# Capacity experts: last products as pairs of 64-row products, gate and up products in two banks

## The chip, the cores and the metric

The kernel runs on one core of a Trainium2 chip. It is a raw program: each engine has its own hand-written instruction order, and waits are explicit semaphores. The metric is the device time of one execution in microseconds (us), lower is better. All data are float32.

## The reference, cut to what matters

The program is four transformer-like layers over 8 sequences of 512 tokens with 128 features. The change touches only the last piece, the expert mixture of layer L3. There are 64 experts with hidden width 64, each takes at most 256 token copies (CAP), and every token goes to its two best experts:

```
buf = zeros(E=64, CAP=256, d=128).at[flat_e, pos].set(x_pairs, mode='drop')
h = silu(einsum('ecd,edh->ech', buf, w1)) * einsum('ecd,edh->ech', buf, w3)      # h = 64
y = einsum('ech,ehd->ecd', h, w2)                                               # contraction over 64
routed = (y[flat_e, pos] * top_scores).sum over the two choices
out = shared + routed
```

## The kernel before

The last layer is the function `capacity_mixture`. It has three stages.

The first routes. For each pair of sequences, the tokens' normalized rows are written to a DRAM array `queues` at expert*256+position by indirect DMAs that GpSimd issues (`scatter`, 64 of them, line 2436). Meanwhile SyncE loads the weights: `w13` (gate and up weights, 4 MB) and `w2_pairs` (4 MB, into `big`, lines 2412 and 2413).

The second is the expert loop. It runs over 32 units u, a unit being two experts (a = 0 and 1) with 256 rows each. Per unit, TensorE does, in this order in iteration u:

- T(u): four transposes of the loaded rows X(u) into bank `XP(u)` (line 2727); ScalarE copies them to `XT` (line 2644).
- G(u-1): gate and up products (line 2736), four matmuls with a 128x64 weight tile and 256 moving columns; expert a writes partitions 64a to 64a+63 of the bank `GU`. ScalarE takes a tanh of the gate half (2650), VectorE multiplies twice (2597 and 2601) and leaves `AA`, whose partitions 0 to 63 are the hidden values of expert 0 and 64 to 127 those of expert 1.
- Y(u-3): the last products (line 2747). Two matmuls, one for each 128 of the 256 slots, each with all 128 partitions of `AA` as the stationary operand and 256 columns of `w2` moving. `w2_pairs` holds the weights padded: the columns of expert 0 are zero in partitions 64 to 127 and those of expert 1 are zero in partitions 0 to 63, so one matmul gives both experts' outputs side by side. VectorE scales by 0.5 out of bank `YP(u)` into `Y(u)` (2593), and GpSimd issues the store to `results` (2452).

`DEEP` = 4 is the number of `GU` banks (2 to 5), `ROOM` = 2 that of the other banks. G(v) waits for AA(v-4), Y(v) for AA(v) and for the scaling of v-2.

The third stage gathers two rows for each token back from `results` (64 indirect DMAs, line 2463), and VectorE adds them with their shares (2561).

In the text an "fp32 matmul" of the program shows in the trace as two MATMUL and two LDWEIGHTS instructions (Y: 2 matmuls, x4 in the rows; G: 4 matmuls, x8); a transpose shows as one.

Of the kernel before, what the change touches and what calls it, by code (L numbers as in the profile page):

```python
# [13 lines left out]
F32 = mybir.dt.float32  # L14
I32 = mybir.dt.int32
U32 = mybir.dt.uint32
ALU = mybir.AluOpType
# [3 lines left out]
P = 128  # L21
B, T, D = 8, 512, 128
NC_ = T // P
NT = B * NC_
# [6 lines left out]
CE, CH, CAP = 64, 64, 256  # L31
# [62 lines left out]
class Memory:  # L94


    def __init__(self, ctx, nc, dram):
        self.ctx, self.nc, self.dram = ctx, nc, dram


        self.h_more = self.sb("h", [P, NT + 2 * NC_, D])
        self.h = self.h_more[:, 0:NT, :]
        self.bank = [ctx.enter_context(nc.psum_tensor(f"bank{n}", [P, T], F32)) for n in range(8)]
        self.w = {}
        self.loaded = {}
        self.load_log = []
# [2229 lines left out]
def capacity_mixture(ctx, nc, m):  # L2336
# [4 lines left out]

    w13 = ctx.sb("w13", [P, CE, 2 * CH])
    w13_in, w2_in = ctx.semaphore("loaded_w13"), ctx.semaphore("loaded_w2")
    w2 = m.big[:, NT * D:NT * D + CE // 2 * 2 * D].rearrange("p (q n) -> p q n", n=2 * D)
    place_of = ctx.sb("place", [P, PAIRS, 4 * NC_])
    share = ctx.sb("share", [P, PAIRS, 4 * NC_])
    idx = ctx.sb("cc_idx", [P, PAIRS, 4 * NC_], I32)
# [33 lines left out]
    sg_ps, su_ps, sg_sb, s1_sb, s2_sb, sy_ps, sh_sb = (sig(n, 2) for n in ("g_ps", "u_ps", "g_sb", "s1_sb", "s2_sb", "y_ps", "h_sb"))  # L2381

    sig = named("ce_")
    UN, SLOTS, DEEP, ROOM = CE // 2, 8, 4, 2
    QC = CAP // P
    X = lambda u: m.KM[0][:, u % SLOTS, :]
    Y = lambda u: m.KM[1][:, u % SLOTS, :]
    XT = lambda u: m.XT[u % 2]
    TH = lambda u: m.t512a[u % 2][:, u // 2 % 2 * CAP:(u // 2 % 2 + 1) * CAP]
    AA = lambda u: m.t512b[u % 2][:, u // 2 % 2 * CAP:(u // 2 % 2 + 1) * CAP]  # L2390
# [2 lines left out]
    x_free, xt_ps, xt_sb, gu_ps, th_sb, a_sb = (sig(n) for n in ("x_free", "xt_ps", "xt_sb", "gu_ps", "th_sb", "a_sb"))  # L2393
    aa_sb, y_ps, y_sb = (sig(n) for n in ("aa_sb", "y_ps", "y_sb"))
    XP = lambda u: m.bank[u % 2]
    GU = lambda u: m.bank[2 + u % DEEP]
    YP = lambda u: m.bank[6 + u % 2]
    acf = lambda v: v.rearrange("p (a c f) -> p a c f", a=2, c=QC)
    rows = lambda t, u: t[u * 2 * CAP:(u + 1) * 2 * CAP, :].rearrange("(a p c) d -> p a (c d)", a=2, c=QC)
    nd = lambda v: v.rearrange("p (a n) -> p a n", a=2)  # L2400

# [5 lines left out]
    with nc.Block() as block:  # L2407
# [60 lines left out]
        def _(dve):  # L2468
# [120 lines left out]
            def last_part(u):  # L2589
                dve.wait_ge(y_ps.sem, u + 1)  # L2590
                if u >= SLOTS:
                    dve.wait_ge(y_out[u % SLOTS].sem, 16 * (u // SLOTS))
                nc.vector.tensor_scalar(acf(Y(u)), YP(u)[:, :].rearrange("p (c a f) -> p a c f", a=2, c=QC), 0.5, None, ALU.mult).then_inc(y_sb.sem, 1)

            for u in range(UN):
                dve.wait_ge(th_sb.sem, u + 1)
# [15 lines left out]
        def _(act):  # L2612
# [26 lines left out]
            for u in range(UN + 1):  # L2639
# [5 lines left out]
                if u >= 1:  # L2645
                    v = u - 1
                    act.wait_ge(gu_ps.sem, v + 1)
                    if v >= DEEP:
                        act.wait_ge(aa_sb.sem, v - DEEP + 1)
                    nc.scalar.activation(TH(v), GU(v)[:, 0:CAP], ACT.Tanh, scale=0.5).then_inc(th_sb.sem, 1)  # L2650

        @block.tensor
        def _(pe):
            def gate(i):
                for s in S if i else ():
                    pe.wait_ge(norms[i % 2].ready.sem, norms[i % 2].ready.at(nth(i), s + 1))
                    if i >= 2:
                        pe.wait_ge(sh_sb.sem, sh_sb.at(i - 2, 2))
                    for c in range(NC_):
                        last = nc.tensor.transpose(TB(i, s)[:, c * P:(c + 1) * P], tiles(i, s)[:, c, :], w["ident"][:, :])  # L2660
                    last.then_inc(gx_ps.sem, 1)
                for s in S:
                    if i:
                        pe.wait_ge(gx_sb.sem, gx_sb.at(i - 1, s + 1))
                    for c in range(NC_):
                        n = s * NC_ + c
                        last = nc.tensor.matmul(LG(i)[:, n * CE:(n + 1) * CE], GX[i % 2][s][:, c * P:(c + 1) * P], w["c_gate"][:, :], start=True, stop=True)
                last.then_inc(lg_ps.sem, 1)

            def count(i):  # L2670
                pe.wait_ge(cu_sb.sem, i + 1)
                if i >= 2:
                    pe.wait_ge(s2_sb.sem, s2_sb.at(i - 2, 2))
                into = ne(COUNT(i)[:, :])
                nc.tensor.matmul(into, w["earlier"][:, :], en(M)[:, :, 1:R9].rearrange("p e n -> p n e"), start=True, stop=False)  # L2675
                nc.tensor.matmul(into, w["ones"][:, 0:P], en(INCL)[:, :, 0:R8].rearrange("p e n -> p n e"), start=False, stop=True).then_inc(pos_ps.sem, 1)  # L2676

            def shared_hidden(i):
                for s in S:
                    if s == 0:  # L2680
                        if i:
                            pe.wait_ge(gx_sb.sem, gx_sb.at(i - 1, 2))
                    else:
                        pe.wait_ge(sc_sb.sem, i + 1)
                    nc.tensor.matmul(SHARED_G(i, s)[:, :], w["sw1"][:, :], GX[i % 2][s][:, :], start=True, stop=True).then_inc(sg_ps.sem, 1)
                for s in S:
                    if s == 1:
                        pe.wait_ge(cst.sem, cst.at(i, 2))
                    nc.tensor.matmul(SHARED_U(i, s)[:, :], w["sw3"][:, :], GX[i % 2][s][:, :], start=True, stop=True).then_inc(su_ps.sem, 1)

            def shared_out(i):
                for s in S:
                    pe.wait_ge(s2_sb.sem, s2_sb.at(i, s + 1))
                    for c in range(NC_):
                        last = nc.tensor.matmul(SHARED_Y(i, s)[:, c * P:(c + 1) * P], SG[s][:, c * P:(c + 1) * P], w["sw2"][:, :], start=True, stop=True)
                    last.then_inc(sy_ps.sem, 1)

            pe.wait_ge(m.loaded["c_gate"], 16)
            gate(0)
            pe.wait_ge(m.loaded["earlier"], 16)  # L2700
            count(0)
            gate(1)
            for name in ("sw1", "sw3", "sw2"):
                pe.wait_ge(m.loaded[name], 16)
            shared_hidden(0)
            shared_out(0)
            gate(2)
            count(1)
            for i in range(1, PAIRS - 1):
                shared_hidden(i)  # L2710
                count(i + 1)
                shared_out(i)
                if i + 2 < PAIRS:
                    gate(i + 2)
            shared_hidden(PAIRS - 1)
            shared_out(PAIRS - 1)
            pe.wait_ge(sh_sb.sem, sh_sb.at(PAIRS - 1, 2))

            pe.wait_ge(w13_in, 16)
            pe.wait_ge(w2_in, 16)  # L2720
            for u in range(UN + 3):
                if u < UN:
                    pe.wait_ge(x_in[u % SLOTS].sem, 16 * (u // SLOTS + 1))
                    if u >= ROOM:
                        pe.wait_ge(xt_sb.sem, u - ROOM + 1)
                    for n in range(2 * QC):
                        last = nc.tensor.transpose(XP(u)[:, n * P:(n + 1) * P], X(u)[:, n * P:(n + 1) * P], w["ident"][:, :])  # L2727
                    last.then_inc(xt_ps.sem, 1)
                if 1 <= u <= UN:
                    v = u - 1  # L2730
                    pe.wait_ge(xt_sb.sem, v + 1)
                    if v >= DEEP:
                        pe.wait_ge(aa_sb.sem, v - DEEP + 1)
                    for k in range(2):
                        for a in range(2):
                            last = nc.tensor.matmul(GU(v)[a * CH:(a + 1) * CH, k * CAP:(k + 1) * CAP], w13[:, 2 * v + a, k * CH:(k + 1) * CH],  # L2736
                                                    XT(v)[:, a * CAP:(a + 1) * CAP], start=True, stop=True)
                            if k == a == 0:
                                last.then_inc(x_free.sem, 1)
                    last.then_inc(gu_ps.sem, 1)  # L2740
                if u >= 3:
                    v = u - 3
                    pe.wait_ge(aa_sb.sem, v + 1)
                    if v >= ROOM:
                        pe.wait_ge(y_sb.sem, v - ROOM + 1)
                    for c in range(QC):
                        last = nc.tensor.matmul(YP(v)[:, c * 2 * D:(c + 1) * 2 * D], AA(v)[:, c * P:(c + 1) * P], w2[:, v, :], start=True, stop=True)  # L2747
                    last.then_inc(y_ps.sem, 1)


# [59 lines left out]
def laid_out(inputs):  # L2810

    a = {k: np.asarray(v) for k, v in inputs.items()}
    row = lambda x: np.ascontiguousarray(x)
    out = dict(shape_constants())
# [25 lines left out]
    p = np.arange(P)  # L2840
# [13 lines left out]
    q = np.arange(B * 8)  # L2854
# [24 lines left out]
        out[n] = row(a["L3_ffn_" + n])  # L2879
    out["w13"] = row(np.concatenate([a["L3_ffn_w1"], a["L3_ffn_w3"]], axis=2).transpose(1, 0, 2).reshape(P, -1))  # L2880
    w2 = a["L3_ffn_w2"].reshape(CE // 2, 2, CH, D)
    pairs = np.zeros((2, CH, CE // 2, 2, D), w2.dtype)
    for e in range(2):
        pairs[e, :, :, e] = w2[:, e].transpose(1, 0, 2)
    out["w2_pairs"] = pairs.reshape(P, -1)
    return out


# [13 lines left out]
```

## Time and profile before

| what | value |
|---|---|
| time, median of 3 runs | 2267.86 us (2266.97 to 2274.65) |
| span of the profiled execution | 2301.6 us |
| mean granted TensorE clock over the span | 0.898 |
| expert loop, first transpose to last scaling | 2125.45 to 2208.96 us |
| instructions of PE, PEld, DVE, ACT, POOL | 11676, 11676, 4911, 1459, 392 |

The profile gives no other time of its own execution than its span, which is 33.7 us above the median of the runs. PE is TensorE's matmuls, PEld its weight loads, DVE VectorE, ACT ScalarE, POOL GpSimd, SP SyncE. A duration of a matmul row is its own latency, neighbours overlap, so groups are timed here from the start of one group to the start of the next. PEclk is the granted clock of TensorE: 1.00 is 2.4 GHz and 0.50 is 1.2 GHz. "128*64 128x256" is a weight tile of 128 rows and 64 columns with 256 moving columns on 128 rows.

### The profile page before, as it was taken

Reading aid. Unit: us, or ns where it says so; the run is one execution under the profiler, and the core shown is the slowest. Engines: PE = TensorE matmul, PEld = TensorE weight load, DVE = VectorE, ACT = ScalarE, POOL = GpSimd, SP = SyncE. Lnnn points to the kernel's source line nnn. Section 1 sums busy time; section 2 is a strip of 40 time slices with the busy share of each in tenths; the row PEclk is TensorE's granted clock in tenths of the full one; section 3 lists DMA queues with packets and bytes.
Section 4 is the critical chain, followed back from the end, with each engine's and each line's share of the span. In section 5 each row is a group of like instructions: output and inputs, shape, how many; then the busy total and the mean of one; then the engine's idle time right before and its main releaser. Section 6 shows DMA issues by size and latency. Waiting matters only on the chain. (4 is left out here: it accounts for less than half of the span.)

```text
span 2301.6 us, 31594 instructions
## 1 busy us (share of the span) xinstructions
PE 1858.3 (81%) x11676; PEld 957.7 (42%) x11676; DVE 1747.6 (76%) x4911; ACT 1317.0 (57%) x1459; POOL 327.8 (14%) x392
## 2 busy tenths in 40 slices
PE   5998998988766688999999999889999888652930
PEld 2565755766421123344433334433344553231620
DVE  3667557667777789999999999999999789763532
ACT  0223122231237999999999999999999612100310
POOL 6000022010343000000000000000000000173256
PEclk9879999787777999999999999999999999776975
DMA  5501000000001100000000000000000000221632
GB/s 163 180 1 38 16 2 14 1 1 1 1 0 35 65 1 1 1 1 1 1 1 1 1 1 1 1 1 1 1 1 1 1 1 0 106 92 53 208 96 73
DMA packets 39658, 67.08 MB, mean 29 GB/s; under 512 B 7744, under 2 KB 27728, under 8 KB 38736
## 3 DMA queue, kind: packets, MB, share of 16 engines
q1 hardware_dynamic: 30768, 41.96, 5.4%
q0 software_dynamic: 8736, 23.10, 3.2%
q8 instruction: 93, 1.52, 0.3%
q14 instruction: 61, 0.50, 0.1%
HBM read 39.87 MB, written 23.07 MB: 27 GB/s over the span
## 5 line engine op out<-in xcount | busy, mean ns | idle before, releaser
L1942 ACT ACTIVATE KM<-KM 128x2048 f32<-128x2048 f32 x290 | 538.9, 1909 | 8.0 <-DVE KM L1765 8.0
L1765 DVE TENSOR_SCALAR KM<-big 128x512 f32<-128x512 f32 x1160 | 480.8, 484 | 38.7 <-PE bank L2080 32.9
L2080 PE MATMUL bank<-KM,w_a_wa 128*32 128x512 f32 x2736 | 379.6, 629 | 91.1 <-ACT KM L1942 69.7
L189 POOL TENSOR_TENSOR nrstd<-nrstd,minus_half 128x4 f32<-128x4 f32 (+1 forms) x80 | 82.4, 1050 | 1745.9 <-DVE nrstd L166 1745.5
L1942 ACT ACTIVATE aa_args<-aa_args 128x2048 f32<-128x2048 f32 x142 | 266.1, 1909 | 1.5 <-DVE aa_args L1765 1.5
L1765 DVE TENSOR_SCALAR aa_args<-big 128x512 f32<-128x512 f32 x568 | 236.3, 484 | 13.8 <-PE bank L2080 13.2
L2080 PE MATMUL bank<-aa_args,w_a_wa 128*32 128x512 f32 x1360 | 188.2, 627 | 42.2 <-ACT aa_args L1942 28.5
L2080 PEld LDWEIGHTS bank<-KM,w_a_wa 128*32 128x32 f32 x2736 | 54.8, 109 | 243.0 <-ACT KM L1942 140.6
L2052 PE MATMUL bank<-XT,rf_wgu 128*128 128x256 f32 x512 | 143.9, 404 | 0.0
L2046 PE MATMUL bank<-XT,rf_wgu 128*128 128x256 f32 x512 | 142.2, 400 | 0.8 <-DVE ST L1837 0.8
L1939 ACT ACTIVATE KM<-big 128x512 f32<-128x512 f32 x208 | 132.8, 717 | 0.0
L2052 PEld LDWEIGHTS bank<-XT,rf_wgu 128*128 128x128 f32 x512 | 88.0, 191 | 96.8 <-issue 77.3
L2046 PEld LDWEIGHTS bank<-XT,rf_wgu 128*128 128x128 f32 x512 | 87.5, 189 | 93.4 <-issue 84.7
L1837 DVE SCALAR_TENSOR_TENSOR ST<-ST,bank 128x512 f32<-128x512 f32 x128 | 87.8, 686 | 43.0 <-ACT ST L1932 42.7
L1932 ACT ACTIVATE ST<-bank 128x512 f32<-128x512 f32 x128 | 75.9, 593 | 46.3 <-PE bank L2052 46.3
L2040 PEld LDWEIGHTS bank<-rf_wd,ST 128*128 128x128 f32 x512 | 62.1, 191 | 51.3 <-issue 48.3
L2040 PEld LDWEIGHTS bank<-rf_wd,t512b 128*128 128x128 f32 x512 | 62.3, 191 | 37.8 <-issue 36.9
L1850 DVE SCALAR_TENSOR_TENSOR h<-bank,rf_w,h 128x128 f32<-128x128 f32 x256 | 77.7, 348 | 0.0
L594 ACT COPY KM<-bank 128x512 f32<-128x512 f32 x32 | 17.2, 593 | 104.5 <-PE bank L754 104.5
L2080 PEld LDWEIGHTS bank<-aa_args,w_a_wa 128*32 128x32 f32 x1360 | 27.2, 109 | 119.3 <-ACT aa_args L1942 69.1
L2040 PE MATMUL bank<-rf_wd,ST 128*128 128x128 f32 x512 | 73.8, 287 | 1.8 <-DVE ST L1843 1.7
L2326 PE MATMUL bank<-big,w_ident 128*128 128x512 f32 x128 | 58.8, 619 | 18.9 <-DVE big L2221 18.9
(405 smaller groups left out, 3120.6 us busy)
## 6 DMA issues: line engine op xcount, KB each, us to landing
queues<-zeros SPq DMA_DIRECT2D x1, 8192.0 KB, 24.1
KM<-queues SPq DMA_DIRECT2D x32, 256.0 KB, 3.0
results<-KM POOLq DMA_DIRECT2D x32, 256.0 KB, 3.4
w<-in_w SPq DMA_DIRECT2D x1, 4096.0 KB
big<-in_w_pairs SPq DMA_DIRECT2D x1, 4096.0 KB
mf_tv<-in_task_W SPq DMA_DIRECT2D x1, 2048.0 KB, 10.4
la_v<-in_task_W SPq DMA_DIRECT2D x1, 2048.0 KB, 8.6
big<-XN SPq DMA_DIRECT2D x8, 256.0 KB, 2.7
```

What stands on the lines that cost most here:

```text
L189: self.nc.gpsimd.tensor_tensor(self.m.nrstd[s][:, 0:self.tiles], self.m.nrstd[s][:, 0:self.tiles], self.m.minus_half[:, 0:self.tiles], ALU ...
L1765: last = nc.vector.tensor_scalar(ARG(n, step)[:, cc, :], KU[:, i * T:(i + 1) * T], q, None, ALU.add)
L1837: nc.vector.scalar_tensor_tensor(TH(e), TH(e), 1.0, GATE(e)[:, :], ALU.add, ALU.mult).then_inc(a1_sb.sem, 1)
L1850: last = nc.vector.scalar_tensor_tensor(h, OUT(e)[:, s * D:(s + 1) * D], WT[:, s, e:e + 1], h, ALU.mult, ALU.add)
L1932: nc.scalar.activation(TH(e), GATE(e)[:, :], ACT.Tanh, scale=0.5).then_inc(th_sb.sem, 1)
L1939: last = nc.scalar.activation(ARG(n, step)[:, cc, :], KU[:, i * T:(i + 1) * T], ACT.Tanh, bias=query(n, step, cc))
L1942: last = nc.scalar.activation(ARG(n, step), ARG(n, step), ACT.Tanh)
L2040: last = nc.tensor.matmul(OUT(e)[:, s * D:(s + 1) * D], AC(e)[:, o:o + P], wd[:, e, a, :], start=a == 0, stop=a == HB - 1)
L2046: last = nc.tensor.matmul(LIFT(e)[:, a * TOK:(a + 1) * TOK], wgu[:, e, 1, a, :], XMT[parity][:, 0:TOK], start=True, stop=True)
L2052: last = nc.tensor.matmul(GATE(e)[:, a * TOK:(a + 1) * TOK], wgu[:, e, 0, a, :], XMT[parity][:, 0:TOK], start=True, stop=True)
L2080: last = nc.tensor.matmul(m.bank[g][32 * cc:32 * cc + 32, :], w["a_wa"][:, 30 - 2 * k:62 - 2 * k], ARG(n, step)[:, cc, :], start=k == 0, s ...
L2326: last = nc.tensor.matmul(OUT[half][:, :].rearrange("p (l d) -> p l d", d=D), w["ident"][:, :], every[:, :, k, :], start=k == 0, stop=k == ...
```

## The change

The four `GU` banks become two (banks 2 and 3), and banks 4 to 7 become two pairs of neighbouring banks for the outputs. Y(v) is now four matmuls instead of two: for each 128 slots, expert 0 uses array rows 0 to 63 (its half of `AA` and its own `w2`), writing the first bank of the pair, and expert 1 uses rows 64 to 127, writing the second bank. The moving operand has 128 columns instead of 256, and the weights are stored without the zeros, 2 MB instead of 4 MB. VectorE reads one pair of banks in one instruction. G(v) waits for AA(v-2) instead of AA(v-4).

```diff
-        self.bank = [ctx.enter_context(nc.psum_tensor(f"bank{n}", [P, T], F32)) for n in range(8)]
+        self.bank = [ctx.enter_context(nc.psum_tensor(f"bank{n}", [P, T], F32)) for n in range(4)]
+        self.bank_pair = [ctx.enter_context(nc.psum_tensor(f"bank_pair{n}", [P, 2, T], F32)) for n in range(2)]
+        self.bank += [pair[:, n, :] for pair in self.bank_pair for n in range(2)]
...
-    w2 = m.big[:, NT * D:NT * D + CE // 2 * 2 * D].rearrange("p (q n) -> p q n", n=2 * D)
+    w2 = m.big[:, NT * D:NT * D + CE // 2 * D].rearrange("p (q n) -> p q n", n=D)
...
-    UN, SLOTS, DEEP, ROOM = CE // 2, 8, 4, 2
+    UN, SLOTS, DEEP, GATED, ROOM = CE // 2, 8, 4, 2, 2
...
-    GU = lambda u: m.bank[2 + u % DEEP]
-    YP = lambda u: m.bank[6 + u % 2]
+    GU = lambda u: m.bank[2 + u % GATED]
+    YP = lambda u: m.bank_pair[u % 2][:, :, 0:QC * D]
...
-                nc.vector.tensor_scalar(acf(Y(u)), YP(u)[:, :].rearrange("p (c a f) -> p a c f", a=2, c=QC), 0.5, None, ALU.mult).then_inc(y_sb.sem, 1)
+                nc.vector.tensor_scalar(nd(Y(u)), YP(u), 0.5, None, ALU.mult).then_inc(y_sb.sem, 1)
...
-                    if v >= DEEP:
-                        pe.wait_ge(aa_sb.sem, v - DEEP + 1)
+                    if v >= GATED:
+                        pe.wait_ge(aa_sb.sem, v - GATED + 1)
...
                     for c in range(QC):
-                        last = nc.tensor.matmul(YP(v)[:, c * 2 * D:(c + 1) * 2 * D], AA(v)[:, c * P:(c + 1) * P], w2[:, v, :], start=True, stop=True)
+                        for a in range(2):
+                            last = nc.tensor.matmul(YP(v)[:, a, c * D:(c + 1) * D], AA(v)[a * CH:(a + 1) * CH, c * P:(c + 1) * P],
+                                                    w2[a * CH:(a + 1) * CH, v, :], start=True, stop=True)
...
-    pairs = np.zeros((2, CH, CE // 2, 2, D), w2.dtype)
-    for e in range(2):
-        pairs[e, :, :, e] = w2[:, e].transpose(1, 0, 2)
-    out["w2_pairs"] = pairs.reshape(P, -1)
+    out["w2_pairs"] = row(w2.transpose(1, 2, 0, 3).reshape(P, -1))
```

TensorE's order in the middle of the expert loop before (KM0 holds X, t512b is `AA`, the last number is how many matmuls):

```order
L2747 MATMUL bank6<-big,t512b0 128x256 x2
L2727 MATMUL bank0<-w_ident_1,KM0 128x128 x4
L2736 MATMUL bank5<-XT1,w13 64x256 x4
L2747 MATMUL bank7<-big,t512b1 128x256 x2
L2727 MATMUL bank1<-w_ident_1,KM0 128x128 x4
L2736 MATMUL bank2<-XT0,w13 64x256 x4
```

The same place in the changed kernel:

```order
L2749 MATMUL bank_pair0<-big,t512b0 128x128 x4
L2728 MATMUL bank0<-w_ident_1,KM0 128x128 x4
L2737 MATMUL bank3<-XT1,w13 64x256 x4
L2749 MATMUL bank_pair1<-big,t512b1 128x128 x4
L2728 MATMUL bank1<-w_ident_1,KM0 128x128 x4
L2737 MATMUL bank2<-XT0,w13 64x256 x4
```

The order of the groups is the same; the last products are four instead of two, with half the columns, and the gate and up products alternate between banks 2 and 3.

TensorE's last rows of the program before:

```order
L2747 MATMUL bank6<-big,t512b0 128x256 x2
L2736 MATMUL bank5<-XT1,w13 64x256 x4
L2747 MATMUL bank7<-big,t512b1 128x256 x2
L2747 MATMUL bank6<-big,t512b0 128x256 x2
L2747 MATMUL bank7<-big,t512b1 128x256 x2
```

and in the changed kernel:

```order
L2749 MATMUL bank_pair0<-big,t512b0 128x128 x4
L2737 MATMUL bank3<-XT1,w13 64x256 x4
L2749 MATMUL bank_pair1<-big,t512b1 128x128 x4
L2749 MATMUL bank_pair0<-big,t512b0 128x128 x4
L2749 MATMUL bank_pair1<-big,t512b1 128x128 x4
```

Here too only the size and number of the last products differ: Y(28) stands in front of G(31), and Y(29), Y(30) and Y(31) follow it.

## Rows read from the trace of the kernel before

**Rows 1.** Chain that ended last, 1985 to 2151: start us, us, what.
```profile
2063.02 21.74 another core or an unknown queue
...
2122.67 2.65 DMA KM<-queues
2125.32 0.14 issue
2125.45 1.94 PE bank L2727 x8
2127.39 1.91 PE bank L2736 x8
```
**Rows 2.** The same chain, 2203 to 2215.
```profile
2203.91 1.04 PE bank L2736 x8
...
2206.28 0.70 DVE KM L2593
2206.98 0.14 issue
2207.12 1.12 PE bank L2747 x4
2208.23 0.02 issue
2208.26 0.70 DVE KM L2593
```
**Rows 3.** Timeline of PE, 2129 to 2134: start us, us, engine, what.
```profile
2130.85 0.66 PE L2727 MATMUL bank<-w_ident,KM 128*128 128x128 f32 x4
2131.44 1.08 PE L2736 MATMUL bank<-XT,w 128*64 128x256 f32 x8
2132.45 1.13 PE L2747 MATMUL bank<-big,t512b 128*128 128x256 f32 x4
2133.42 0.60 PE L2727 MATMUL bank<-w_ident,KM 128*128 128x128 f32 x4
2133.95 0.44 PE L2736 MATMUL bank<-XT,w 128*64 128x256 f32 x2
```
**Rows 4.** Timeline of all engines, 2160.5 to 2166.5.
```profile
2162.59 1.13 PE L2747 MATMUL bank<-big,t512b 128*128 128x256 f32 x4
2162.71 0.38 ACT L2650 ACTIVATE t512a<-bank 128x256 f32<-128x256 f32 x1 [0.44 <-PE bank L2736]
2163.13 0.42 DVE L2597 SCALAR_TENSOR_TENSOR t512a<-t512a,bank 128x256 f32<-128x256 f32 x1 [1.03 <-ACT t512a L2650]
2163.58 0.42 DVE L2601 TENSOR_TENSOR t512b<-t512a,bank 128x256 f32<-128x256 f32 x1
2163.92 0.68 DVE L2593 TENSOR_SCALAR KM<-bank 128x512 f32<-128x512 f32 x1
```
**Rows 5.** Tile bank, 2132 to 2204: durations ns min/median/max, first and last start.
```profile
L2727 PE MATMUL bank<-w_ident,KM x112: 272/273/273, 2133.4 to 2201.6; 128*128 128x128 f32 x112
```
**Rows 6.** Timeline of PE, 88.9 to 91.1 (layer L0).
```profile
89.11 0.94 PE L754 MATMUL bank<-t512a,ST 32*128 32x128 f32 x12
89.97 1.09 PE L671 MATMUL bank<-w_ident,XN 128*128 128x128 f32 x8
```
**Rows 7.** Timeline of PEld, 88.9 to 90.2, and line 754's weight loads (min/median/max ns).
```profile
89.11 0.75 PEld L754 LDWEIGHTS bank<-t512a,ST 32*128 32x128 f32 x12 [0.17 <-issue]
...
L754 PEld LDWEIGHTS bank<-t512a,ST x96: 181/187/267, 84.5 to 218.4; 32*128 32x128 f32 x96
```
**Rows 8.** Timeline of PE, 440 to 470 (layer L1).
```profile
444.73 9.64 PE L1401 MATMUL bank<-KM,t512b 32*128 32x256 f32 x48 [1.69 <-DVE big L1077]
```
**Rows 9.** Windows: length, busy us (instructions) of PE, PEclk, DMA share, GB/s.
```profile
85.00:95.00 10.00, 10.00 (x101) 1.00 0.15 51
...
446.50:456.80 10.30, 10.30 (x86) 0.50 0.01 2
```
**Rows 10.** Timeline of PE, 105 to 166 (layer L0).
```profile
137.74 1.65 PE L754 MATMUL bank<-ST 32*128 32x128 f32 x12
139.32 1.97 PE L775 MATMUL bank<-w_ident,mf_x 128*128 128x128 f32 x8
```
**Rows 11.** Windows: length, busy us of PE, PEld, DVE, ACT, POOL, PEclk, DMA share, GB/s.
```profile
2010.00:2020.00 10.00, 8.48 (x49) 5.79 (x47) 9.59 (x39) 2.87 (x5) 5.93 (x6) 1.00 0.98 418
2020.00:2030.00 10.00, 5.44 (x24) 5.06 (x24) 9.79 (x53) 1.77 (x3) 8.25 (x8) 0.68 0.18 64
...
2170.00:2180.00 10.00, 10.00 (x66) 6.65 (x64) 5.78 (x12) 3.88 (x8) 2.81 (x5) 1.00 0.66 211
```

More of the change, by code:

```diff
@@ L2395, in capacity_mixture @@
     XP = lambda u: m.bank[u % 2]
-    GU = lambda u: m.bank[2 + u % DEEP]
-    YP = lambda u: m.bank[6 + u % 2]
-    acf = lambda v: v.rearrange("p (a c f) -> p a c f", a=2, c=QC)
+    GU = lambda u: m.bank[2 + u % GATED]
+    YP = lambda u: m.bank_pair[u % 2][:, :, 0:QC * D]
     rows = lambda t, u: t[u * 2 * CAP:(u + 1) * 2 * CAP, :].rearrange("(a p c) d -> p a (c d)", a=2, c=QC)
```

## The prediction

> **What bounds the kernel now.** I read the chain that ended last first, because it says which engine's time is the program's. From 2125.45 on it goes through TensorE alone [rows 1], unit after unit, up to G(31); then it passes ScalarE and VectorE once, Y(31), a scaling and a store, and the gathers start [rows 2]. So the expert loop is TensorE's, and what a unit takes there counts once for each unit. The timeline of PE gives the parts, from group start to group start [rows 3]: Y to T is 2133.42 - 2132.45 = 0.97 us, T behind Y is 0.53, G is 2132.45 - 2131.44 = 1.01. That makes 2.51 us a unit, and TensorE never idles. The windows agree: 10.00 of 10.00 us busy, at clock 1.00, VectorE 5.78 and ScalarE 3.88 [rows 11]. The 112 transposes behind a Y are 28 groups, in 68.2 us, that is 27 periods and a bit: 2.51 again [rows 5].
>
> **The change, part by part.**
>
> *Y itself.* The full-array Y takes 0.97 us. No 64-row tile stands in the trace. The nearest is line 754: six matmuls (x12) with 32-row tiles, 128 weight columns and 128 moving columns, that alternate between two row groups and two banks, as the new Y does with 64 rows. Its group takes 89.97 - 89.11 = 0.86 us, entered from a group of 64-column tiles and left into full-array transposes [rows 6], the same two neighbours that Y has. Its twelve weight loads begin within 0.75 - 0.19 = 0.56 us [rows 7]; one load lasts 0.19. If the loads go one by one, eleven steps give 0.05 us each; in pairs, five steps of 0.11. Either way two instructions cost 0.11 us or less, so the new Y, eight instructions, is 0.86 - 2 x 0.11 = 0.64 us: 0.33 less than now.
>
> *What follows Y.* Before, T followed Y in the same 128*128 shape and took 0.53 us. Now it follows another shape. T behind G, which also changes shape, takes 2131.44 - 2130.85 = 0.59 [rows 3]. So T costs 0.06 more. The drain in front of T is already in the 0.64, since rows 6 are measured up to the next group's start.
>
> On the change of shape, the rows show that 0.06 and whatever stands in the 0.86. The Trainium skill, "TensorEngine Tiling (Array Packing)", section Key Properties, says that changing the tiling mode drains the engine, which speaks against this change: it makes three changes a unit out of two. By this trace the whole price is inside the numbers above.
>
> *Sum of a unit.* 0.64 + 0.59 + 1.01 = 2.24 us against 2.51, 0.27 less. 28 units have a Y and a T behind it: 28 x 0.27 = 7.6 us. Y(28) is followed by G(31), which changes shape anyway: 0.33. Y(29) and Y(30) lie beside the ScalarE and VectorE work behind G(31), and cost nothing on the path; cover gone, they would cost 0.64 each, but the scaling that Y(31) waits for comes after the last multiplication in any case [rows 2]. Y(31) is on the path, 0.33 less. The total is 8.2 us less.
>
> *Two GU banks instead of four.* G(v+2) now waits for AA(v). Counting from a Y start that follows G(v), AA is there at 2163.58 + 0.42 - 2162.59 = 1.41 us [rows 4]. G(v+2) begins two periods less one G later, 2 x 2.24 - 1.01 = 3.47 us. The wait has 2.06 us of room and costs nothing. Behind the waiting G would stand Y, then T and so ScalarE's copy; they get no later. If the room were gone, each late 0.1 us of AA would cost 3.0 us over 30 units.
>
> *VectorE.* The scaling reads 512 values from PSUM now from two banks instead of one; I take its 0.68 us. VectorE does 0.42 + 0.42 + 0.68 = 1.52 us a unit, which the 1.03 us of idle time in front of it [rows 4] shrinks to 0.76 at 2.24. Not a bound; for that the scaling would have to take twice as long.
>
> *Transfers.* A unit loads and stores 0.52 MB; at 2.24 us that is 236 GB/s against 211 now at a DMA share of 0.66 [rows 11]: some 0.74, and eight X buffers lie ahead. Hidden. The weight load is 2 MB shorter, some 5 us at 418 GB/s, but the load is over in the window before 2030 anyway [rows 11] and TensorE needs it at 2125: nothing.
>
> Bounds of the unknown, the row-tiled Y. Below: four pair steps of 0.11 = 0.45 and T at its old 0.53, so 1.99 a unit, 0.52 less, 15.6 us in all. Above: the tiles do not overlap, next rival. I take 0.64, since rows 6 are the same shape but for the rows used.
>
> **The rivals.**
>
> *The halves do not run together (slightly slower).* Line 754's group needs 0.86 - 0.56 = 0.30 us beside its steps [rows 6, 7]; eight instructions one after the other are seven steps of 0.11 more, 1.07 us, 0.10 above the old Y, and T is still 0.06 more: +0.16 a unit, +4.5 over 28 and 0.2 for Y(28) and Y(31), about 2273. For it: no 64-row tile is in the trace. Against it: rows 6 and 7. It decides from a Y group of 0.91 us on, where the gain is gone. The weight loads are the likeliest cause: their number doubles. The Trainium skill, "TensorE: Matmul & The Clock Gate", section LDWEIGHTS, says that a load costs by its columns, not its rows, about 107 ns for 128, so that eight one by one would be 0.85 us (an estimate from that page) and would leave no gain; by rows 7 loads of two row groups overlap, and four pairs are the count.
>
> *The clock falls (clearly slower).* In layer L1, 48 instructions of 32-row tiles in a row took 9.64 us [rows 8] with TensorE busy all the time, at clock 0.50 [rows 9]. So a busy TensorE that uses part of its rows can have the low clock, 1.2 GHz. At 0.50 G is 1.91 us, T 0.97 (1.94 for two) [rows 1], and the new Y, from 139.32 - 137.74 = 1.58 for twelve [rows 10] less two steps at twice 0.11, is 1.14: 4.02 a unit, +1.51 over 28, some 2310. It decides from 15% of the units on. Against it: the stretch 85 to 95 in layer L0, with line 754 and others of that shape between full ones, held 1.00 [rows 9], and here the two halves together use all rows and Y is only 0.64 of 2.24.
>
> *The unnamed wait before the loop changes.* For 21.7 us from 2063 the chain waits for something it cannot name [rows 1], while GpSimd scatters. If the shorter weight load took that away, the time would be some 20 us less, about 2240 with the loop's gain. Against it: the load was over before 2030, more than 30 us earlier [rows 11].
>
> *The full gain.* If changing shape costs nothing, 15.6 us less, 2252.
>
> **How the numbers follow.** The profile's span should go from 2301.6 to 2293.4, and the runs, which lie 33.7 us below the profile, from 2267.9 to 2259.7, 0.36% less. Chances: forecast 0.74 (its own range 2255 to 2264), halves not together 0.09 (2273), clock 0.06 (2310), unnamed wait 0.06 (2240), full gain 0.05 (2252). The range 2252 to 2273 leaves out the clock and the unnamed wait, 0.12. What a measurement of this kernel can tell from no change is about 0.5%, 11.3 us; the forecast lies inside it. Faster by more: unnamed wait 0.06, full gain 0.05, and 0.07 of the forecast's edge: 0.18. Slower by more: the clock, 0.06. The rest, 0.76, is within.
>
> **What would show it.** Line 2749 groups begin 0.64 us before the T behind them, in pairs of close starts; T behind Y 0.59; period 2.24; clock 1.00 from 2130 to the end of the loop; TensorE still busy 10.00 of 10.00 with no wait for `AA`; VectorE's scaling 0.68 us; first gather some 8 us earlier, behind a loop that begins at the same time. Wrong would be: a Y of 0.9 or more, a second level of the clock in the loop, or another start of the loop.

## The result, and the profile after

The changed kernel takes 2264.38 us (median of 20 runs) against 2271.05 for the kernel before: ratio 0.9975, 95% interval 0.9966 to 0.9984, so 3.6 to 7.7 us faster. The quotient of the two medians is 0.9971, inside that interval. Forecast were 8.2 us less, 0.9964 and a time of 2259.7 us. Two repeats gave 0.9971 (0.9959 to 0.9983) and 0.9967 (0.9947 to 0.9988).

The timeline of PE of the changed kernel, from its first transpose on, answers to [rows 1] and [rows 3]:

```profile
2095.42 1.94 PE L2728 MATMUL bank<-w_ident,KM 128*128 128x128 f32 x8 [19.61 <-DMA KM<-queues]
2097.29 1.98 PE L2737 MATMUL bank<-XT,w 128*64 128x256 f32 x8
...
2102.43 0.71 PE L2749 MATMUL bank_pair<-big,t512b 64*128 64x128 f32 x8
2103.07 0.66 PE L2728 MATMUL bank<-w_ident,KM 128*128 128x128 f32 x4
2103.66 1.08 PE L2737 MATMUL bank<-XT,w 128*64 128x256 f32 x8
2104.68 0.71 PE L2749 MATMUL bank_pair<-big,t512b 64*128 64x128 f32 x8
2105.32 0.66 PE L2728 MATMUL bank<-w_ident,KM 128*128 128x128 f32 x4
```

Read from start to start: Y 2103.07 - 2102.43 = 0.64 us (0.97 before), T 0.59 (0.53), G 1.02 (1.01). The period is 2104.68 - 2102.43 = 2.25 us against 2.51. The lines of the other engines in one unit, to be held against [rows 4]:

```profile
2113.66 0.72 PE L2749 MATMUL bank_pair<-big,t512b 64*128 64x128 f32 x8
2113.72 0.71 POOL L2453 DMA_DIRECT2D results<-KM  x1 [1.54 <-DVE KM L2594]
2113.78 0.38 ACT L2651 ACTIVATE t512a<-bank 128x256 f32<-128x256 f32 x1 [0.44 <-PE bank L2737]
2114.20 0.42 DVE L2598 SCALAR_TENSOR_TENSOR t512a<-t512a,bank 128x256 f32<-128x256 f32 x1 [0.77 <-ACT t512a L2651]
...
2114.65 0.42 DVE L2602 TENSOR_TENSOR t512b<-t512a,bank 128x256 f32<-128x256 f32 x1
...
2114.99 0.68 DVE L2594 TENSOR_SCALAR KM<-bank_pair 128x512 f32<-128x512 f32 x1
```

VectorE's idle time in front of its first product has shrunk from 1.03 to 0.77 us, and its instructions last as long as before: the scaling out of two banks takes the same 0.68 us. A window of the loop (columns as in [rows 11]):

```profile
2120.00:2130.00 10.00, 10.00 (x94) 6.25 (x90) 6.01 (x14) 4.35 (x10) 3.42 (x5) 1.00 0.72 235
```

TensorE is still busy all the time, at clock 1.00; the DMA share is 0.72.

**The two spans don't tell the gain.** The profiled spans are 2301.6 us before and 2261.7 after, 39.9 us apart, and most of that has nothing to do with the change. The 64 scatters and the 64 gathers, before and then after (min/median/max ns, first and last start):

```profile
L2436 POOL DMA_INDIRECT queues<-big,cr_sidx x64: 956/962/1366, 2015.1 to 2120.4; - x64
L2463 POOL DMA_INDIRECT KM<-results,cc_idx x64: 943/947/1027, 2212.7 to 2291.7; - x64
```
```profile
L2437 POOL DMA_INDIRECT queues<-big,cr_sidx x64: 954/958/1371, 2005.5 to 2090.3; - x64
L2464 POOL DMA_INDIRECT KM<-results,cc_idx x64: 940/945/1092, 2174.8 to 2253.7; - x64
```

The first scatter already comes 9.6 us sooner, and so does the issue of the weight load (1989.74 against 1999.31), which is the first instruction that differs. A second profile of the changed kernel has its first scatter at 2011.8, so this part varies without any change. The scatters take 105.3 us in one and 84.8 in the other: that is the unnamed wait of [rows 1]. Only what lies between the first transpose and the first gather is the change: 2212.68 - 2125.45 = 87.2 us before, 2174.77 - 2095.42 = 79.35 after, 7.9 us less. In the tables below this stretch is called loop time.

The end of the loop after, from the chain that ended last, answers to [rows 2]:

```profile
2166.05 1.04 PE bank L2737 x8
...
2168.42 0.70 DVE KM L2594
2169.12 0.28 issue
2169.40 1.42 POOL results L2453 x2
2170.82 0.17 issue
2170.99 2.89 DMA results<-KM
```

What follows the scaling of Y(29) at 2168.42 is now GpSimd, which issues the stores of units 29 and 30 one after the other in 1.42 us, and then the last one. The chain passes Y(31) by, but only just: the last scaling starts at 2170.01, 0.98 us before the last store is issued, and in the kernel before it was 0.98 us too (2208.26 to 2209.24). The last scaling and the last store of the changed kernel (timeline), then the last store of the kernel before (chain):

```profile
2170.01 0.69 DVE L2594 TENSOR_SCALAR KM<-bank_pair 128x512 f32<-128x512 f32 x1 [0.30 <-PE bank_pair L2749]
2170.99 0.71 POOL L2453 DMA_DIRECT2D results<-KM  x1 [0.17 <-issue]
```
```profile
2208.96 0.28 issue
2209.24 2.54 DMA results<-KM
```

From issue to landing the last store took 2.54 us and now takes 2.89. So from the last scaling's start to the first gather it was 4.42 us (2208.26 to 2212.68) and is 4.76 (2170.01 to 2174.77).

### The profile page after: what moved, and what is told of

It is laid out like the page before. It is cut to its first block and busy times, and to the rows that moved or that the text cites. A ratio compares the mean times of both kernels' runs of the same rounds, so it can differ in the third digit from the quotient of the medians.

```text
span 2261.7 us, 31852 instructions
## 1 busy us (share of the span) xinstructions
PE 1845.4 (82%) x11804; PEld 950.2 (42%) x11804; DVE 1746.0 (77%) x4911; ACT 1316.9 (58%) x1459; POOL 328.4 (15%) x392
## 5 line engine op out<-in xcount | busy, mean ns | idle before, releaser
L2048 PE MATMUL bank_pair<-XT,rf_wgu 128*128 128x256 f32 x320 | 88.3, 398 | 0.8 <-DVE ST L1839 0.8
L2054 PE MATMUL bank_pair<-XT,rf_wgu 128*128 128x256 f32 x320 | 88.2, 398 | 0.0
L2042 PEld LDWEIGHTS bank_pair<-rf_wd,ST 128*128 128x128 f32 x512 | 62.1, 191 | 51.3 <-issue 48.3
L596 ACT COPY KM<-bank_pair 128x512 f32<-128x512 f32 x32 | 17.2, 593 | 105.1 <-PE bank_pair L756 105.1
L2042 PEld LDWEIGHTS bank_pair<-rf_wd,t512b 128*128 128x128 f32 x512 | 62.3, 191 | 37.8 <-issue 36.9
L2048 PEld LDWEIGHTS bank_pair<-XT,rf_wgu 128*128 128x128 f32 x320 | 54.8, 189 | 54.2 <-issue 48.6
L1852 DVE SCALAR_TENSOR_TENSOR h<-bank_pair,rf_w,h 128x128 f32<-128x128 f32 x256 | 77.0, 341 | 0.0
L2054 PEld LDWEIGHTS bank_pair<-XT,rf_wgu 128*128 128x128 f32 x320 | 54.4, 189 | 52.8 <-issue 36.0
L2042 PE MATMUL bank_pair<-rf_wd,ST 128*128 128x128 f32 x512 | 73.8, 287 | 1.8 <-DVE ST L1845 1.7
L2328 PE MATMUL bank_pair<-big,w_ident 128*128 128x512 f32 x128 | 58.8, 619 | 18.9 <-DVE big L2223 18.9
L2042 PE MATMUL bank_pair<-rf_wd,t512b 128*128 128x128 f32 x512 | 72.3, 284 | 0.0
L1941 ACT ACTIVATE aa_args<-big 128x512 f32<-128x512 f32 x112 | 71.4, 716 | 0.0
```

Of the source, the lines that this page charges most:

```text
L1852: last = nc.vector.scalar_tensor_tensor(h, OUT(e)[:, s * D:(s + 1) * D], WT[:, s, e:e + 1], h, ALU.mult, ALU.add)
L1941: last = nc.scalar.activation(ARG(n, step)[:, cc, :], KU[:, i * T:(i + 1) * T], ACT.Tanh, bias=query(n, step, cc))
L2042: last = nc.tensor.matmul(OUT(e)[:, s * D:(s + 1) * D], AC(e)[:, o:o + P], wd[:, e, a, :], start=a == 0, stop=a == HB - 1)
L2048: last = nc.tensor.matmul(LIFT(e)[:, a * TOK:(a + 1) * TOK], wgu[:, e, 1, a, :], XMT[parity][:, 0:TOK], start=True, stop=True)
L2054: last = nc.tensor.matmul(GATE(e)[:, a * TOK:(a + 1) * TOK], wgu[:, e, 0, a, :], XMT[parity][:, 0:TOK], start=True, stop=True)
L2328: last = nc.tensor.matmul(OUT[half][:, :].rearrange("p (l d) -> p l d", d=D), w["ident"][:, :], every[:, :, k, :], start=k == 0, stop=k == ...
```

## The experiments

Each is compared with the kernel before on the same chip, except one half, which has a single run. After the first result there were three comparisons, each on another chip; the kernel before took 2271, 2292 and 2298 us in them.

| kernel | ratio to before, 95% interval | loop time, us | scatters, us |
|---|---|---|---|
| before, first profile | | 87.2 | 105.3 |
| before again | 1.0009, 0.9984 to 1.0034 | 88.3 | 99.5 |
| before, two gate banks | 1.0004, 0.9991 to 1.0017 | 87.2 | 84.8 |
| before, two by two | 0.9998, 0.9976 to 1.0021 | 85.2 | 101.3 |
| changed | 0.9975, 0.9966 to 0.9984 | 79.4 | 84.8 |
| changed, second time | 0.9971, 0.9959 to 0.9983 | 79.3 | 84.8 |
| changed, third time | 0.9967, 0.9947 to 0.9988 | 80.3 | 99.8 |
| changed, halves in turn | 0.9976, 0.9961 to 0.9990 | 80.5 | 84.8 |
| changed, long load | 0.9947, 0.9925 to 0.9969 | 79.6 | 101.3 |
| changed, long load, second time | 0.9968, 0.9942 to 0.9993 | 79.3 | 105.2 |
| changed, one half (one run) | | 79.7 | 101.0 |
| changed, two by two | 0.9949, 0.9933 to 0.9965 | 73.7 | 84.8 |
| changed, two by two, second time | 0.9947, 0.9922 to 0.9972 | 73.5 | 105.1 |

Two loop times among those near 79.4 stand out. With the halves in turn (80.5) the last store took 3.81 us to land instead of 2.89. In the changed kernel's third profile (80.3) the clock rose later, so that its third and fourth group took 1.04 and 1.53 us instead of 0.61 and 1.02.

**The changed kernel again.** Expected:

> The changed kernel itself, once more. If the gain is the expert loop's alone, the profile again has a period of 2.25 us, a loop that ends 8.2 us sooner after its own start than in the profile of before (2125.45 to 2208.96), and the runs are 7.9 us faster (0.65 us of the loop's and the tail's difference being given back at most). If something outside the loop gives back part of it, the runs stay near 5.7 us. The 20 us wait in the scatters of the first profile: if the shorter weight load removed it, it is absent in this profile as in the first one of the changed kernel; if it comes and goes, it says nothing.

The loop is the same to 0.1 us, and the runs gave 6.6 us less. The scatters' wait is absent again, but see the next one.

**Two gate banks alone.** The edit in the kernel before:

```diff
-    UN, SLOTS, DEEP, ROOM = CE // 2, 8, 4, 2
+    UN, SLOTS, DEEP, GATED, ROOM = CE // 2, 8, 4, 2, 2
...
-    GU = lambda u: m.bank[2 + u % DEEP]
+    GU = lambda u: m.bank[2 + u % GATED]
...
-                    if v >= DEEP:
-                        pe.wait_ge(aa_sb.sem, v - DEEP + 1)
+                    if v >= GATED:
+                        pe.wait_ge(aa_sb.sem, v - GATED + 1)
```

> The kernel before with only one part of the change: gate and up products in two banks, G(v) waits for AA(v-2). My theory: the wait has about 2 us of room, so the loop's period stays 2.51 us and the time is within 2 us of before. Rival: the wait bites, TensorE shows idle time in front of the gate products and the period grows; at 0.1 us a unit that is 3 us.

Loop time 87.2 as before and a ratio of 1.0004: the two banks cost nothing in the loop, and nothing in the time that the interval (2 us less to 4 us more) can show. The timeline of PE of this kernel:

```profile
2105.95 1.13 PE L2747 MATMUL bank<-big,t512b 128*128 128x256 f32 x4
2106.91 0.60 PE L2727 MATMUL bank<-w_ident,KM 128*128 128x128 f32 x4
2107.44 1.08 PE L2736 MATMUL bank<-XT,w 128*64 128x256 f32 x8
2108.46 1.13 PE L2747 MATMUL bank<-big,t512b 128*128 128x256 f32 x4
```

2.51 us from Y to Y, no idle time. It also has the padded 4 MB load, and its scatters took 84.8 us: so the unnamed wait does not belong to that load.

**The halves in turn.** The edit in the changed kernel:

```diff
-                    for c in range(QC):
-                        for a in range(2):
+                    for a in range(2):
+                        for c in range(QC):
```

> The changed kernel with the four last products in another order: both of expert 0 (rows 0 to 63) and then both of expert 1, so that row groups alternate once and not at each matmul. If only neighbours of different row groups overlap, then most of the eight instructions go one after the other: a last-product group of about 1.0 us instead of 0.64, period about 2.6 us, some 10 us slower than the changed kernel, 2 us or more slower than before. If the overlap comes from the smaller tiles whatever their order, the group stays 0.64 and the time is that of the changed kernel.

It is the changed kernel's time: 2163.12 to 2163.77 is 0.65 us for a Y group in its chain, and the ratio is 0.9976. My expectation of 1.0 us fell. The order leaves open whether row groups overlap in any order, or whether a 64-row instruction is simply cheap. The next kernel tells these apart.

**One half alone.** The edit in the changed kernel, which leaves out expert 1's last products and with them half of the routed outputs:

```diff
-                        for a in range(2):
+                        for a in range(1):
                             last = nc.tensor.matmul(YP(v)[:, a, c * D:(c + 1) * D], AA(v)[a * CH:(a + 1) * CH, c * P:(c + 1) * P],
```

> The changed kernel without expert 1's last products: only the two matmuls of rows 0 to 63 are left of each four (half of the routed outputs are left out). It asks how the eight instructions of the last products come to 0.64 us. Theory: two row groups run side by side, each instruction takes 0.11 us in its own. Then four instructions of one group take as long as the eight of two, the group stays about 0.64 us and the period 2.25. Rival, which the unchanged time of the other order allows: a 64-row instruction costs 0.055 us by itself, whatever runs beside it; then the group falls to about 0.42 us and the period to 2.03.

The timeline of PE of this kernel:

```profile
2142.00 0.71 PE L2749 MATMUL bank_pair<-big,t512b 64*128 64x128 f32 x4
2142.64 0.66 PE L2728 MATMUL bank<-w_ident,KM 128*128 128x128 f32 x4
2143.23 1.08 PE L2737 MATMUL bank<-XT,w 128*64 128x256 f32 x8
2144.24 0.71 PE L2749 MATMUL bank_pair<-big,t512b 64*128 64x128 f32 x4
```

Four instructions of one row group take the same 0.64 us as eight of two. An instruction is not cheap by itself; the second half costs nothing because it runs beside the first. Windows of 0.08 and 0.1 us inside one Y group, of line 2749 alone, with the count of instructions under way (in brackets, PE first), bear it out, for one half:

```profile
2142.05:2142.15 0.10, 0.10 (x1) 0.10 (x2) 1.00 0.55 225
```

and for the halves in turn:

```profile
2109.00:2109.10 0.10, 0.10 (x2) 0.10 (x4) 1.00 1.00 410
2109.20:2109.28 0.08, 0.08 (x4) 0.08 (x4) 1.00 0.04 0
```

Right at the start of its group the kernel with the halves in turn has two matmuls under way where one half has one (the changed kernel has two as well). The rows don't say which expert a matmul belongs to. But expert 0's four instructions alone never put a second one under way there, so the second is taken to be expert 1's: it did not wait for the end of expert 0's, although it stands behind all of them in the program.

**The long load.** The edit in the changed kernel:

```diff
-    w2 = m.big[:, NT * D:NT * D + CE // 2 * D].rearrange("p (q n) -> p q n", n=D)
+    w2_more = m.big[:, NT * D:NT * D + CE // 2 * 2 * D]
+    w2 = w2_more[:, 0:CE // 2 * D].rearrange("p (q n) -> p q n", n=D)
...
-            sp.dma_start(w2.rearrange("p q n -> p (q n)"), m.dram["w2_pairs"]).then_inc(w2_in, 16)
+            sp.dma_start(w2_more, m.dram["w2_pairs"]).then_inc(w2_in, 16)
...
-    out["w2_pairs"] = row(w2.transpose(1, 2, 0, 3).reshape(P, -1))
+    out["w2_pairs"] = row(np.concatenate([w2.transpose(1, 2, 0, 3).reshape(P, -1), np.zeros((P, CE // 2 * D), w2.dtype)], axis=1))
```

> The changed kernel with the weight load of the last products padded back to 4 MB by zeros behind the weights, which nothing reads. If the load's size matters to the time, or if it decides the 20 us wait that the first profile of before shows in the scatters, this kernel is slower than the changed one by some us and may show that wait. My theory: the load is over long before it is needed, the time is that of the changed kernel within 2 us, and the wait is absent.

It ran on another chip, where before took 2292.36 us instead of 2271. The ratio of 0.9947 would be 12 us, more than the changed kernel had brought, but its loop time is 79.6 us. So it was put beside the changed kernel in one comparison:

> The changed kernel a third time. From its first transpose to the first gather it took 79.4 us in both profiles, 7.9 us less than the 87.2 of before, yet the runs showed 5.7 and 6.6 us. If the loop's gain is the whole effect, the ratio is near 0.9965 and the three results together cover it. If about 2 us are given back outside the loop, it is near 0.9975 again.

> The changed kernel with the 4 MB load again, now beside the changed kernel in one comparison. On the chip of its first run it was 12 us faster than before, with a wait in the scatters that all four kernels of that call showed. If the load's size does nothing, its ratio equals that of the changed kernel within 0.002. If the shorter load costs something in the stage before the loop, this one is the faster of the two by 2 us or more.

0.9967 and 0.9968. The length of the load does nothing that these intervals, some 5 us to each side, can see; the loop times are 80.3 and 79.3, apart by the clock at the start as said above. And the 0.9947 before was more than the loop can give; it is not explained. The wait in the scatters was there, 99.8 and 105.2 us.

**Before again.** On the chip of the first long load:

> The kernel before itself, as a measure of what no change looks like: a ratio of 1.000 with an interval of about 0.0015 to each side. Its profile shows whether the 21.7 us wait in the scatters belongs to this kernel: if yes, it is there again; if it comes and goes, it is absent and the span is near 2270 us.

The ratio is 1.0009, with an interval of 0.0025 to each side where 0.0015 was expected, and the scatters took 99.5 us. The wait is in all seven profiles of the two slower comparisons and in none of the four of the first, whatever the kernel: it goes with the chip or the time of the run, not with the change.

**Two units at a time.** TensorE's loop of the changed kernel, with the same three steps as functions:

```diff
-            for u in range(UN + 3):
...
+            for j in range(0, UN + 4, 2):
+                for step, lag in ((turn, 0), (gate_up, 2), (down, 4)):
+                    for v in (j - lag, j - lag + 1):
+                        if 0 <= v < UN:
+                            step(v)
```

> The changed kernel with TensorE's loop over two units at a time: T T, G G, Y Y instead of T, G, Y. Tile shapes change three times for two units instead of six. By the rows: T T 0.59 + 4 x 0.109 = 1.03, G G 1.01 + 0.86 = 1.87, Y Y 0.64 + 0.45 = 1.09, together 3.99 us for two units against 4.50, so 0.25 us less a unit, about 8 us less than the changed kernel and 14 to 16 less than before. Rival: the bursts make TensorE wait for AA or XT, since G of the second unit needs VectorE's last product sooner; then idle time shows in front of G and the gain is less than half of that.

> The two-by-two order with 64-row last products again, beside the changed kernel in one comparison. From the first transpose to the first gather its profile showed 73.7 us against 79.4. Theory: 5.7 us faster than the changed kernel, ratio to before near 0.994. Rival: the gain over the changed kernel is chance, then it is within 2 us of it.

2259.63 us and a ratio of 0.9949, and in the second comparison 0.9947. It beats the kernel before. Against the changed kernel beside it the medians are 5.2 us lower (2259.63 and 2264.78) and 7.6 us lower (2281.9 and 2289.46); the intervals of the two kernels overlap, a little in the first comparison and more in the second, so the size of this gain is loose. The loop times are 5.7 and 6.8 us apart. Its timeline of PE, from the start and in the middle of the loop:

```profile
2096.81 1.94 PE L2727 MATMUL bank<-w_ident,KM 128*128 128x128 f32 x8 [19.52 <-DMA KM<-queues]
2099.32 1.78 PE L2727 MATMUL bank<-w_ident,KM 128*128 128x128 f32 x8 [0.57 <-DMA KM<-queues]
2101.03 1.95 PE L2736 MATMUL bank<-XT,w 128*64 128x256 f32 x16
2103.16 0.63 PE L2727 MATMUL bank<-w_ident,KM 128*128 128x128 f32 x4 [0.19 <-ACT XT L2645]
...
2110.45 1.16 PE L2748 MATMUL bank_pair<-big,t512b 64*128 64x128 f32 x16
2111.54 1.09 PE L2727 MATMUL bank<-w_ident,KM 128*128 128x128 f32 x8
2112.57 1.95 PE L2736 MATMUL bank<-XT,w 128*64 128x256 f32 x16
2114.44 1.16 PE L2748 MATMUL bank_pair<-big,t512b 64*128 64x128 f32 x16
```

2114.44 - 2110.45 = 3.99 us for two units, as worked out, and no idle time in the middle. The loop time is 73.7, so 5.7 us less than the changed kernel and not 8. The 8 us counted a saving for every unit, but from the first pair of last products (2106.46) to the last pair that has transposes in front of it (2158.37) there are 13 periods, worth 13 x 0.51 = 6.6 us. At the start TensorE waits 0.57 us for the second pair's transfer and 0.19 and 0.23 us for ScalarE's copies, with only half of the first units' work behind it. At the end it waits 0.20, 0.44 and 0.77 us for VectorE, where the changed kernel waits once, 1.05 us.

The same order in the kernel before:

> The kernel before (full-array last products, padded weights, four gate banks) with the two-by-two order T T, G G, Y Y. By the rows: T T behind Y of the same shape 0.53 + 4 x 0.109 = 0.97, G G 1.87, Y Y 0.97 + 4 x 0.215 = 1.83, together 4.67 us for two units against 5.03, 0.18 us less a unit: about 5.5 us less than before. That is less than the 11.6 us of the same order with row tiles, so the two parts add up. Rival: the order alone is what brought the 11.6 us, then this one gets near it.

Its period is 4.68 us, worked out as 4.67 (from its timeline):

```profile
2136.45 1.99 PE L2746 MATMUL bank<-big,t512b 128*128 128x256 f32 x8
2138.28 1.04 PE L2726 MATMUL bank<-w_ident,KM 128*128 128x128 f32 x8
2139.25 1.95 PE L2735 MATMUL bank<-XT,w 128*64 128x256 f32 x16
2141.13 1.99 PE L2746 MATMUL bank<-big,t512b 128*128 128x256 f32 x8
```

but the loop time is 85.2, only 2.0 to 3.1 us less than before, and the ratio 0.9998 shows no gain; its interval, some 5 us to each side, can't tell 2 us from none. The two-unit start costs most of the rest (the window's columns as in [rows 11]):

```profile
2120.24 1.94 PE L2726 MATMUL bank<-w_ident,KM 128*128 128x128 f32 x8 [18.90 <-DMA KM<-queues]
2122.74 1.97 PE L2726 MATMUL bank<-w_ident,KM 128*128 128x128 f32 x8 [0.55 <-DMA KM<-queues]
2124.64 3.65 PE L2735 MATMUL bank<-XT,w 128*64 128x256 f32 x16
```
```profile
2124.70:2128.20 3.50, 3.50 (x17) 1.66 (x16) 0.84 (x2) 0.86 (x2) 0.00 (x0) 0.51 0.47 149
```

Sixteen gate and up instructions took 3.65 us here at the clock's low level, where in the other kernel they took 1.95. When the clock rises is not the same in every execution (before again has a loop time of 88.3 instead of 87.2 us; its third group, a T, took 1.04 us instead of 0.61), so a part of this is chance. In the profiles at least, the order alone does not bring what it brings together with row tiles: with them each unit has three changes of shape to save on, without them two.

## Why the prediction was right, point by point

The mechanism came out as forecast, term by term. The number did so less well: 2264.38 us lies just outside the forecast's own range (2255 to 2264) and inside the wide one.

- **The new Y, 0.64 us.** Measured 0.64. The 32-row group of layer L0 with the same neighbours [rows 6, 7] carried over to 64 rows to the hundredth. I did not need to know there whether its instructions ran in pairs; one half alone shows that two row groups run side by side, at 0.11 us an instruction in each.
- **T behind another shape, 0.06 more.** Measured 0.59 against 0.53. The third change of shape costs this and the drain inside the 0.64. The two-by-two order, which halves the changes, took 3.99 us for two units instead of 4.50.
- **28 units and two more Ys, 8.2 us.** From the first transpose to the last scaling's start it was 2208.26 - 2125.45 = 82.8 us and is 74.6 (2170.01 - 2095.42): 8.2 us less. This sum was right, with small errors that cancel: up to Y(28) it was 7.4 us (forecast 7.6), for Y(28) 0.4 and from G(31) to the last scaling 0.4 (0.33 each).
- **The tail.** Here the prediction left something out. It credited 0.33 us for Y(31) and carried the store and the first gather over unchanged. But the last store takes 2.89 us to land instead of 2.54, and so 0.34 us are given back; the loop time fell by 7.9 us. This is no chance of one profile: from the last scaling's start to the first gather it is 4.4 us in all four profiles with full-array last products, 4.7 to 4.9 in eight with 64-row ones and 5.7 in the ninth. GpSimd's pause before this store has shrunk from 0.55 to 0.17 us, so the last stores follow each other more closely and may share the queue's time; no run tried that.
- **Two GU banks, VectorE, transfers: nothing.** Right, by the kernel with two gate banks (1.0004), the unchanged 0.68 us of the scaling, and DMA share 0.72 (forecast 0.74) with TensorE busy throughout.
- **The rivals.** The halves do run together, whatever their order. Behind the start of the loop the clock stayed 1.00. The unnamed wait does not depend on the load. Changing shape is not free.
- **A sign of being wrong that came.** "Another start of the loop" was one, and the loop did start 30.0 us sooner (2095.42 against 2125.45). It did not come from the change: 20.5 us of it are the scatters' wait, which is absent from the kernel with two gate banks too and present in later profiles of the changed kernel, and 9.6 us lie before the first scatter.
- **The size.** 7.9 us would be a ratio of 0.9965. The three measurements gave 0.9975, 0.9971 and 0.9967; the second and third intervals hold 0.9965, the first ends just short of it at 0.9966. No stage of the profiles is seen to give back the 1 to 2 us that lie between, but the stage before the first scatter differs by 6.3 us between two profiles of the changed kernel, so the profiles can't rule it out. Whether they are there at all stays open. Of the 4.7 us between the forecast time of 2259.7 and the 2264.38 measured, 3.2 are the kernel before itself: its median was 2267.86 in three runs and 2271.05 in twenty. And the 11.3 us that the prediction took as the least a measurement can tell were too many: the intervals here reach 2 to 6 us to each side.

The prediction also took the 33.7 us between the first profile and the runs shown as a property of profiling. The later comparisons suggest another reason: the kernel before had a median of 2292 and 2298 us on the chips whose profiles show the scatter wait, and 2271 where they don't, and a run whose profile was taken had a span 1.0 to 1.9 us below its own time. So the first profile, with that wait in it, is probably of a slower execution than the three runs beside it; its own time is not on record.

## What to carry to other kernels

If a contraction fills only half of the array's rows, look in the same trace for any group with row tiles and the same neighbours: its time from start to start already contains the drains and prices the change. Zero-padding two products into one full-array matmul moves twice the columns, here 0.97 us a group against 0.64; giving it up paid although it added a change of tile shape for each unit. Once shapes alternate, try putting groups of one shape together (with row tiles it paid, in the kernel before it brought nothing that could be measured), and count the start and the end of the loop as well as its period.

## What the runs showed of the hardware that I had not expected

The order of the two row groups in the program did not matter: two matmuls of each expert in turn overlapped as fully (0.65 us a group) as matmuls that alternate, where I had expected about 1.0.

```profile
2084.78 0.60 ACT L2622 ACTIVATE KM<-bank 128x512 f32<-128x512 f32 x1 [21.20 <-remote]
```

While GpSimd issued the scatters, ScalarE sometimes stood still for a long time, 21.2 us in the first profile of before (the row above) and up to 21.8 in others. The matmuls that this instruction reads from had ended at 2065.61. The wait was there in some comparisons in every profile and in others in none (scatter stage 99.5 to 105.3 us against 84.8), with the same instructions. The stage is 14.7 to 20.5 us longer with it, about twice the loop's gain of 7.9 us or more. What holds ScalarE is not known; no run here tried it.
